# A hand-written order of steps for the engines of a fused transformer block: a second order for the same steps

## The reference

```python
h = L0_tok(x, W, b)                       # two Haar levels, resize to 8 x 8, 7 maps -> 64 values
h = concat([h, txt], axis=1)              # 16 x 192 x 64
h = h + L0_attn(layernorm(h))             # plain self-attention, one head of 64
h = h + L0_ffn(layernorm(h), ...)         # routed: of 192 tokens the 95 with the largest weight
                                          # get gelu(x w1 + b1) w2 + b2, times that weight; "+ x" for all
h = h + L1_attn(layernorm(h), ...)        # 16 query heads, one key/value head, rotary, rms norm,
                                          # window of 128, softmax, output projection
h = h + L1_ffn(layernorm(h), ...)         # argmax over 32 experts, two small layers with relu
```

## Time and profile before

| what | value |
|---|---|
| median of 3 runs | 582.63 us (580.71 to 585.87) |
| the profiled execution | 583.62 us |
| its span in the trace | 581.8 us |
| busy PE / DVE / ACT / POOL | 502.2 / 417.8 / 311.9 / 234.7 us |

### The profile page before, as it was taken

How to read it: one execution, slowest core, us unless ns; L and a number is a source line. 1 busy time by engine, 2 the same in 40 slices (tenths; PEclk the granted TensorE clock), 3 DMA queues, 4 the chain that set the end, 5 groups by cost and what they waited for, 6 DMA issues and landing times.

```text
span 581.8 us, 14569 instructions
## 1 busy us (share of the span) xinstructions
PE 502.2 (86%) x5920; PEld 386.4 (66%) x5920; DVE 417.8 (72%) x1291; ACT 311.9 (54%) x593; POOL 234.7 (40%) x217
## 2 busy tenths in 40 slices
PE   3457499879999899989998999899989999899845
PEld 2235277658867786778776877688767767777622
DVE  3669766996799769976997699957995697363220
ACT  1414346565667556766577565756575655454311
POOL 2316632554446342643454436354462446420000
PEclk9999999989999999999998999899999999999966
DMA  7000000000000000000000000000000000000000
GB/s 271 1 6 0 1 7 2 3 1 7 3 2 10 7 2 2 10 7 3 2 9 3 2 3 2 8 3 2 3 10 2 2 2 9 2 3 9 2 1 7
DMA packets 6450, 6.29 MB, mean 11 GB/s; under 512 B 4208, under 2 KB 5744, under 8 KB 6256
## 3 DMA queue, kind: packets, MB, share of 16 engines
q1 hardware_dynamic: 6384, 5.37, 3.0%
HBM read 4.31 MB, written 0.79 MB: 9 GB/s over the span
## 4 chain that ended last, share of the span: by engine, by line
PE 47%; DVE 35%; ACT 9%; POOL 2%; issue 2%; DMA 2%; SPq 1%; POOLq 0%; ACTq 0%; DVEq 0%
PE bank L961 38%; PE bank L979 10%; DVE eq L515 5%; DVE negm L631 4%; DVE q_sb L568 4%; DVE ssq L585 4%; DVE tb L568 4%; DVE on L648 3%; ACT qT L810 3%; POOL qs L793 2%; DMA p<-masks 2%; DVE eq L506 1%; ACT qs L810 1%; DVE eq L431 1%; DVE rec L644 1%
## 5 line engine op out<-in xcount | busy, mean ns | idle before, releaser
L631 DVE TENSOR_REDUCE negm<-bank 128x2 f32<-128x384 f32 (+1 forms) x128 | 79.2, 619 | 39.6 <-PE bank L961 38.4
L793 POOL TENSOR_TENSOR qs<-q_sb,qs 128x1024 fp32r<-128x1024 f32 x24 | 56.8, 2368 | 107.8 <-ACT qs L810 107.8
L919 ACT ACTIVATE p<-bank 128x512 f32<-128x512 f32 x112 | 66.0, 599 | 56.6 <-PE bank L961 55.4
L961 PE MATMUL bank<-kh,qT 128*128 128x128 f32 (+1 forms) x384 | 82.0, 323 | 0.0
L810 ACT ACTIVATE qT<-bank 128x512 fp32r<-128x512 f32 x96 | 54.3, 596 | 50.3 <-PE bank L979 49.9
L961 PE MATMUL bank<-vx,p 128*64 128x65 f32 x1536 | 68.8, 225 | 1.3 <-DVE on L648 1.2
L961 PEld LDWEIGHTS bank<-vx,p 128*64 128x64 f32 x1536 | 60.5, 138 | 13.9 <-issue 6.8
L756 POOL TENSOR_TENSOR q_sb<-q_sb,tb 128x512 f32<-128x512 f32 x24 | 36.5, 1519 | 74.3 <-DVE tb L568 74.3
L961 PEld LDWEIGHTS bank<-kh,qT 128*128 128x128 f32 x384 | 64.2, 199 | 2.1
L961 PE MATMUL bank<-sh_r,sh_l 128*128 128x512 f32 x112 | 53.2, 475 | 0.0
L644 DVE RECIPROCAL rec<-bank 128x4 f32<-128x4 f32 (+1 forms) x88 | 15.7, 179 | 48.4 <-PE bank L961 48.0
(11 more groups left out here) (158 smaller groups left out, 1122.9 us busy)
## 6 DMA issues: line engine op xcount, KB each, us to landing
wts<-weights SPq DMA_DIRECT2D x1, 1313.5 KB, 7.3
h<-txt SPq DMA_DIRECT2D x1, 672.0 KB, 8.4
img<-images SPq DMA_DIRECT2D x8, 72.0 KB, 1.9
q_sb<-wqkv SPq DMA_DIRECT2D x1, 576.0 KB, 9.7
sh_r<-mT SPq DMA_DIRECT2D x32, 4.0 KB
out<-o_sb SPq DMA_DIRECT2D x8, 64.0 KB, 1.9
p<-masks SPq DMA_DIRECT2D x1, 480.0 KB, 10.4
cst<-shapes SPq DMA_DIRECT2D x1, 304.0 KB, 3.8
```

Source lines behind the costliest of these rows:

```text
L631: ve.tensor_reduce(dst, src, AX_X, ALU.max, negate=True).then_inc(s_vec, 1)
L793: gp.tensor_tensor(qs[:, :, D:2 * D], ta[:, t, 0:NH, :], qs[:, :, 0:D].bitcast(F32), ALU.subtract).then_inc(b_pool, 1)
L919: ac.activation(dst.rearrange("s h t -> s (h t)"), bank[BANK_E[n % 2]][:, :], ACT.Exp).then_inc(e_act, 1)
L961: return pe.matmul(dst, lhsT, rhs, start=start, stop=stop, skip_group_check=True)
```

## The change

In the first stretch VectorE runs, before, `A.ctx.1 B.kv.0 A.ln2.1 B.sq21.0 B.sqk.0 B.rms.0 A.xn2.1 B.kk.0 A.rank1.1 A.rank2.1 A.rank3.1`, and after, `A.ctx.1 A.ln2.1 B.kv.0 B.sq21.0 B.sqk.0 A.xn2.1 B.rms.0 A.rank1.1 B.kk.0 A.rank2.1 A.rank3.1`. The diff, cut (the strings of GpSimd and SyncE are whole, of the others the beginning):

```diff
 MERGE = {
-    "pe": "A15 B4 A B A B A B A B A2 B2 A2 B2 A S A B A B S A S B S B2 S A S B A S E2 S B2 A S B2 V S B A S B V S B "
+    "pe": "A15 B4 A B A B A B A B A3 B2 A2 B2 S B2 S A S A B S A B S B S B E S A V S A S A B S A S B2 E S B V S B E "
...
-    "ac": "A4 W4 A5 B3 A B A B2 A B2 A2 B3 A2 B2 A B6 S A B2 A E2 B2 A B2 S B2 E B E2 B E2 V B V S E B A B A B A E A "
+    "ac": "A4 W4 A5 B3 A B A B2 A B2 A3 B3 A B5 A B2 S B3 E A3 B S B2 E B2 E A2 B A B E A B E3 S A V B V E B2 E2 B E "
...
-    "ve": "W A4 W A W A7 B A B A2 B A B10 A B A B3 A B A5 B S A S A2 S A S4 B S V A S B S V B S B V S B S A S B V S "
+    "ve": "W A4 W2 A8 B A B A2 B A B10 A2 B3 A B A B A3 S A B S2 A S A3 S2 V B S2 A S A S V A S B S V A B S B3 S A S "
...
-    "gp": "A W3 A2 B A B4 A B2 A B4 A B3 A B A B7 A B D B2 A2 B9 A B D B2 A2 B9 A B D B2 A2 B9 A B D B2 A2 B9 A B D "
-          "B2 A2 B10 D B12 D B D",
-    "sp": "A3 S3 A S3 D A S3 D A S3 D S3 D S3 D S3 D S3 D2 A2",
+    "gp": "A W3 A2 B A B3 A B A B6 A B2 A2 B2 A B6 A B A B2 D B2 A B6 A B A B4 D B A B6 A2 B4 D B2 A B6 A2 B4 D B2 A "
+          "B6 A2 B4 D B13 D B10 D B D",
+    "sp": "A3 S2 A S2 A S2 D S2 A S D S3 D S3 D S3 D S3 D S3 D2 A2",
 }
```

## The result

The changed kernel took 578.31 us (median of 6 runs, 577.46 to 578.59), the one before 582.49 (6 runs, 580.71 to 585.87): a ratio of 0.992, 95% interval 0.989 to 0.995, or 4.2 us less. That is within 1%. Forecast was 568.1 with a range of 560.5 to 581.5: the time lies inside the range, the size is off by 10 us. The profiled execution took 578.6 with a span of 576.8, 5.0 less than before. Lines of after are those of before plus one.

The account below looks back on a forecast made before the run. TensorE was taken to bound the middle, idle mainly before X2 because A.rank2 stands behind GpSimd. The terms -11.2 - 3.7 - 2.7 - 2.5 - 1.4 + 0 + 5.0 + 2.0 = -14.5 gave 568.1 us, range 560.5 to 581.5.

Parts of the forecast that it names:

- (1): TensorE's six waits before X2 for VectorE's V7, late behind A.rank2, go: -11.2 us.
- (2): TensorE's clock: three of four falls, which come after long waits before X2, go: -3.7 us.
- (3): Pair 0: TensorE's waits before A.xT2 (1.55 us) and V7 (1.18) go: -2.7 us.
- (4): Smaller waits: S2's for S1's maximum, and ScalarE's table loads, 21 for 29: -2.5 us, from -1.7 to -6.
- (5): The start: kk.0 comes about 2 us later, but tq10.0 about 1.4 us earlier: -1.4 us, from -3 to +2.
- (6): A work runs further ahead, into the first stretch: 0, or +2.4 us if the last pairs don't give it back.
- The costs: TensorE's new waits: before S3, +5.0 us over five pairs; at tq00 and mT1, +2.0, from 0 to +6.
- C: Rival: only the X2 waits go, clock falls remain, last pairs don't give back the A work: 576 us, chance 0.15.
- D: Rival: kk's cast is locked behind GpSimd too, V7 comes 1.9 us later: 575 us, chance 0.06.
- A: Rival: the S chain eats most of the gain, one further full lock in each of five pairs: 580 us, chance 0.15.
- B: Rival: the lock moves onto S and falls twice a pair: 592 us and more, slower than before, chance 0.06.

Follow-up runs that it names:

- e1: Kernel before, with V7 put ahead of A.rank2 on VectorE in pairs 0 to 5: 573.4 us, ratio 0.985.
- e8: Kernel before, with A.rank2's compare-and-multiply made a maximum with one SBUF source, ties not counted: 567.9 us, ratio 0.976.
- e10: Kernel before, with TensorE's waits in the tail of pair 7 filled by matmuls that nothing reads: 577.4 us, ratio 0.993.
- e2: Changed kernel, with B.kk.0 put ahead of A.rank1.1 on VectorE: 575.2 us, ratio 0.988 to the kernel before.
- e6: Changed kernel, with kk.0 ahead of A.rank1.1, S2 ahead of A.rank1 and S7 ahead of B.xs in several pairs, S6.0 and S7.0 ahead of B.xs.1: 571.4 us.
- e3: Changed kernel, with 8 unread matmuls behind B.kv.0 and 8 behind A.h1a.1 in TensorE's early waits: 575.4 us, ratio 0.988 to the kernel before.
- e9: Changed kernel, with A.rank2's compare-and-multiply made a maximum with one SBUF source, ties not counted: 577.1 us, ratio 0.992 to the kernel before.
- e5: Changed kernel, with S2 ahead of A.rank1 in three pairs and S7 ahead of B.xs in four, on VectorE: 574.9 us, ratio 0.988 to the kernel before.

## Why the prediction was off

What bounds the kernel, and the lock as the mechanism, held: e1 and e8 are 8.6 and 14.1 us faster for it.

(1) The wait before X2, -11.2, is gone in all pairs, as the steps of the forecast had it: kk stood half behind m0 (1.03 us for the subtraction in pair 3) and V7 came in time. (2) Of the four falls of the clock none is left between pairs 0 and 5; but the clock rose 5 us later at the start and fell 9 us earlier by the time axis (549.7 against 558.4, of which 5 is the shorter run), so that wo2.7 ran partly at the half clock. The term had looked only at the falls in the middle. It also counted one execution: e10's trace, whose order is that of before up to its tail, has a single fall between 90 and 550 us, at 372.5, where before's has four. (3) The two waits of pair 0 (-2.7) went, though V5.0 waits 0.82 and S7.0 1.35 where before had none above 0.3. With the first two terms they make the 5.9 us gained between 94 and 134, where some 7 were expected. (4) The 21 table loads came exactly; S2's wait of the steady pairs is not there in after, and the one before S3, 0.33, is of the same size.

**The step that failed is (5), the start, with what I left out behind it.** Forecast was -1.4, and +3.3 came (4.7 of the 10 us). Up to tq10.0 the step went nearly as worked out: kTh.0 came 2.6 us later (69.05 for 66.46; forecast 2), tq00.0 at 74.50 (73.9), tq10.0 0.9 us earlier (1.4). But the lock on A.rank1.1 was priced too low: e2, which takes kk.0 out from behind it, gains 3.2 us against the 2 of the forecast. And the sum stopped at tq10.0 and took the head start there for time gained. It was not: the work that before does from 84 to 94 us takes after 13.5 us (priced by single instruction here, which moves the table's numbers by up to 0.7). 0.9 of these 3.5 us are more waiting, above all the 1.35 before S7.0; the rest is slower matmuls, at the half clock until 92.3 where before had the full one from 87.3. For this I had no term. It takes 13.5 us in e2 too (12.4 in e6, where the wait before S7.0 is gone), so the late kk.0 is not its cause; e2 stands at +0.1 only because it comes to it 3.2 us earlier. Why the clock rises later in the new weave, and what an earlier rise alone would give, stays open (e3).

**The passage from pair 0 to pair 1 had no term at all.** It costs 2.2 to 2.3 us between 134 and 160 in all four kernels with the new weave (after, e2, e6, e9) and nothing in e1 and e8. A.rank2's lock is not its cause, since e9 has none; the four waits shown sum to 2.4. Which change of the strings would remove it was not tried. I had written out the weave of the steady pairs and taken it for the others. The same holds for pairs 1 and 2: from 160 to 254 two of X2's waits (3.6 in the forecast) and S2's, less the costs, should have given some 1.5 us, and 0.4 came. e9 against e8 puts 3.1 us of the new weave's price there; no run takes it apart.

(6) A further ahead was put at 0, or +2.4 should the last pairs not give it back. They lose 0.8 instead of gaining the 1.8 of X2.5's wait less its costs. Each order has small waits of its own there, after among them 1.25 before wo1.5, 0.74 before tq20.6, 0.62 before tq00.7 and 0.79 before S5.7. No run takes this apart.

**The costs** were of the right kind and too high in the steady pairs: S3 0.33 for 1.0, mT1 0.4 and tq00 0.2 for 0.4 together. e5 puts the first two at 0.75 a pair in all, against 1.4 forecast. Two steady pairs gained 5.0 us (from 254 to 381) where X2 3.6, the clock 2.4 and S2 0.7, less 2.8, give 3.9.

In all, -14.1 is what A.rank2's lock was worth (e8; the forecast's first three terms had -17.6), +9.2 what the new weave costs besides (e9 over e8; the forecast's other terms had +3.1), and +1.3 what A.rank2's old form still costs in it (after over e9). These three are steps from before to after and so must sum to their difference: -3.6, or -3.7 from the medians, with the before of those groups at 582.0; the -4.2 of the result is against 582.5.

**The rivals.** C, only the X2 waits go and the last pairs give nothing back, at 576, is nearest in time, but its clock did not fall in the middle. D did not occur: kk's cast took 0.54 to 0.55 us under a running m0 each time it is shown. The Trainium skill's page "SBUF — State Buffer", section "Who interferes with whom", says of a cast that it can enter a mode that takes the shared port, if its operands allow it; this one was never held. A and B, the lock on S, did not occur: only A.rank1's first product stands under lo1 (1.06 us for 0.28, from A.rank1.5 on), as the forecast had placed it. The loss by a late start had no rival of its own, only a bound of +2 in the term, and that the time still lies in the range is owed to the room left for A and C.

## What to carry to other kernels

Before a long order is rewritten for one stall, exchange the two steps at the stall alone: here that got 8.6 us where the full new weave got 4.2. In a hand-woven schedule the steady state is the easy part; write out the first pair, the passage to the second and the last with the same care, and ask for each step that is put under a long GpSimd instruction who is queued behind it. When a tail is a chain of short matmul steps with waits between, look at its granted clock before looking at its waits.

## What was unexpected in the hardware

A small instruction with two sources in SBUF can be held for as long as one GpSimd instruction runs: the three of A.rank1.1 took 0.54, 1.97 and 1.98 us under m0 and m1, which took 3.86 together (0.28 to 0.29 free). A TENSOR_REDUCE over the same columns was never held (332 to 353 ns for each of 32). Matmuls that compute nothing, put into waits of 0.6 to 3.4 us, kept the granted clock at its full level from 375.9 to the end of e10's span at 573.9, while the tail of before ran at the half level from 558.4 to 578.8; in the first 70 us, 16 of them did not keep it up (e3, at half again from 72.3 to 89.4).
